# Middle attention layer of a four-layer graph network: the folds of a chunk's sums on GpSimd in place of VectorE

## The reference

```python
def _gat_layer(x, W, a_s, a_d, b, src, dst, n):
    h = x @ W
    logits = leaky_relu(h[src] @ a_s + h[dst] @ a_d, 0.2)
    m = segment_max(logits, dst, num_segments=n)
    e = exp(logits - m[dst])
    denom = segment_sum(e, dst, num_segments=n)
    coef = e / (denom[dst] + 1e-16)
    return segment_sum(coef[:, None] * h[src], dst, num_segments=n) + b
```

## Time and profile before

| what | value |
|---|---|
| median of 3 runs | 2841.45 us (2840.66 to 2842.64) |
| profiled execution, its own time | 2841.15 us |
| its span | 2838.9 us |
| TensorE busy | 2431.0 us, 86% |
| VectorE busy | 2203.5 us, 78% |
| ScalarE busy | 1548.5 us, 55% |
| GpSimd busy | 424.0 us, 15% |
| mean granted TensorE clock | 0.942 of full |

### The profile page before, as it was taken

How to read it: one execution, slowest core, us unless ns; L and a number is a source line. 1 busy time by engine, 2 the same in 40 slices (tenths; PEclk the granted TensorE clock), 3 DMA queues, 4 the chain that set the end, 5 groups by cost and what they waited for, 6 DMA issues and landing times. The chain is left out here.

```text
span 2838.9 us, 86445 instructions
## 1 busy us (share of the span) xinstructions
PE 2431.0 (86%) x31023; PEld 2188.3 (77%) x31024; DVE 2203.5 (78%) x4979; ACT 1548.5 (55%) x1943; POOL 424.0 (15%) x921
## 2 busy tenths in 40 slices
PE   2656999999999679999599998769999868999998
PEld 2644777677777569988599888669999858898997
DVE  8986899898899879999799899799999984222212
ACT  6004444444444289998799987588888740000101
POOL 1003555555556300000000000000000000000000
PEclk8877999999999889999899999989999979999999
DMA  3003443533435347676356655225655437888998
GB/s 107 0 0 87 127 127 88 166 87 108 145 87 149 99 160 266 234 265 215 104 189 205 226 181 181 91 92 183 204 181 181 158 115 247 308 306 299 330 366 299
DMA packets 398046, 494.28 MB, mean 174 GB/s; under 512 B 81925, under 2 KB 397289, under 8 KB 397674
## 3 DMA queue, kind: packets, MB, share of 16 engines
q1 hardware_dynamic: 364760, 487.44, 51.0%
q10 hardware_dynamic: 33044, 3.63, 1.0%
HBM read 401.81 MB, written 89.17 MB: 173 GB/s over the span
## 5 line engine op out<-in xcount | busy, mean ns | idle before, releaser
L2740 PE MATMUL psum<-sb_arena 128*128 128x99 bf16 (+2 forms) x13524 | 1011.3, 236 | 127.7 <-DVE sb_arena L2010 82.6
L2740 PEld LDWEIGHTS psum<-sb_arena 128*128 128x128 f16 x13524 | 969.7, 99 | 157.2 <-DVE sb_arena L2010 103.0
L3366 ACT ACTIVATE sb_arena<-sb_arena 128x896 f16 (+1 forms) x980 | 961.7, 1036 | 152.4 <-PE psum L2740 107.4
L2000 DVE TENSOR_TENSOR sb_arena<-sb_arena 128x896 f16<-128x896 f16 x980 | 593.0, 621 | 84.9 <-ACT sb_arena L3366 55.2
L3035 ACT ACTIVATE sb_arena<-psum 128x784 f16<-128x784 f32 x392 | 322.5, 823 | 394.6 <-PE psum L2385 226.5
L1280 DVE TENSOR_SCALAR sb_arena<-sb_arena 128x392 f16<-128x392 f16 x1960 | 486.9, 323 | 0.0
L2385 PE MATMUL psum<-sb_arena 64*128 64x392 f16 x3920 | 387.0, 341 | 70.1 <-ACT sb_arena L3035 25.0
L2835 PE MATMUL psum<-sb_arena 128*128 128x192 bf16 x4802 | 416.2, 248 | 30.4 <-DVEq L2157 15.2
L2835 PEld LDWEIGHTS psum<-sb_arena 128*128 128x128 f16 x4802 | 402.5, 98 | 46.0 <-DVEq L2157 16.1
L2010 DVE TENSOR_TENSOR sb_arena<-sb_arena 128x896 f16<-128x896 f16 x686 | 424.0, 618 | 0.3
L2385 PEld LDWEIGHTS psum<-sb_arena 64*128 64x128 bf16 x3920 | 258.3, 138 | 151.3 <-issue 79.8
(11 more groups left out here) (381 smaller groups left out, 1444.5 us busy)
## 6 DMA issues: line engine op xcount, KB each, us to landing
sb_arena<-counts SPq DMA_DIRECT2D x245, 896.0 KB, 6.9
sb_arena<-counts SPq DMA_DIRECT2D x245, 672.0 KB, 4.6
counts<-sb_arena SPq DMA_DIRECT2D x56, 1344.0 KB, 6.7
sb_arena<-records SPq DMA_DIRECT2D x392, 5.0 KB, 2.1
sb_arena<-records ACTq DMA_DIRECT2D x392, 5.0 KB, 2.2
counts<-sb_arena SPq DMA_DIRECT2D x1, 5488.0 KB, 19.8
records<-sb_arena SPq DMA_DIRECT2D x1, 3124.0 KB, 8.9
counts<-sb_arena SPq DMA_DIRECT2D x14, 112.0 KB, 4.6
```

The costliest lines, as they stand in the source:

```text
L2000: nc.vector.tensor_tensor(above_at[r % RING], above_at[r % RING], counts_of(g, j), ALU.mult).then_inc(above_ready, 1)
L2740: last = nc.tensor.matmul(psum[:, bank, at:at + wide], of[:, b * BLK:(b + 1) * BLK], moves[side][:, r, 0:wide], start=(r == 0 and at == 0) ...
L3366: nc.scalar.activation(above_at[r % RING], of, ACT.Sigmoid, bias=steep_s[:, r:r + 1], scale=STEEP).then_inc(signs_ready, 1)
```

## The change

GpSimd does steps 0 to 6 of the fold for the sums of chunks 0 to 5 (`fold_levels` in its own stream, the same arithmetic in 14 instructions with 9 drains), between the waits for phase 9 and phase 10, as soon as ScalarE has copied the banks out. It raises a new semaphore `folded`. VectorE no longer does these steps; in the middle layer it waits for `folded` at row MEAN_AT = 20 and does step 7 there, and step 8 at row 21. TURN_AT goes from 17 to 23, KEEP_AT from 24 to 28, MIX_AT from 26 to 30 and OUT_AT from 33 to 35. The fold of chunk 6, after the layer's end, stays whole on VectorE, and so do the folds of the first and third layers.

```diff
-TURN_AT = 17
-KEEP_AT = 24
-MIX_AT = 26
-OUT_AT = 33
+MEAN_AT = 20
+TURN_AT = 23
+KEEP_AT = 28
+MIX_AT = 30
+OUT_AT = 35
...
-                for k in range(9, 13):
-                    phase_end(pool, k)
+                def add_pieces(l, c):
...
+                    pool.wait_ge(banks_kept, c * len(groups) + (banks_before(l) + len(groups)))
+                    nc.gpsimd.tensor_tensor(kept4[:, :, 0], kept4[:, :, 0], kept4[:, :, 1], ALU.add)
+                    pool.drain()
+                    nc.gpsimd.tensor_tensor(kept4[:, :, 0], kept4[:, :, 0], kept4[:, :, 2], ALU.add)
+                    pool.drain()
+                    return kept4
...
+                def fold_levels(c):
+                    kept4 = add_pieces(1, c)
...
+                        nc.gpsimd.tensor_tensor(side, side, v.unsqueeze(2).broadcast_to([BLK, CB, wd]), ALU.mult)
+                    first, later_sums, lows = kept4[:, 0:2 * CB:2, 0], kept4[:, 1:2 * CB:2, 0], kept4[:, 2 * CB:3 * CB, 0]
+                    nc.gpsimd.tensor_scalar(picked[:, 0, :], first[:, :, fw], 0.0, None, ALU.is_gt)
+                    nc.gpsimd.tensor_scalar(picked[:, 1, :], first[:, :, fw], 0.0, None, ALU.is_equal)
+                    pool.drain()
+                    for q in range(2):
+                        nc.gpsimd.tensor_tensor(picked[:, 2 + 2 * q:4 + 2 * q, :], of_chunk(levels[:, 1 + 2 * q:3 + 2 * q, :]),
+                                                picked[:, q, :].unsqueeze(1).broadcast_to([BLK, 2, CB]), ALU.mult)
+                    scaled_by(first, of_chunk(levels[:, 0:1, :])[:, 0, :])
+                    pool.drain()
+                    nc.gpsimd.tensor_tensor(picked[:, 2:4, :], picked[:, 2:4, :], picked[:, 4:6, :], ALU.add)
+                    pool.drain()
+                    for q in range(2):
+                        scaled_by(later_sums, picked[:, 2, :])
+                        scaled_by(lows, picked[:, 3, :])
+                        pool.drain()
+                    nc.gpsimd.tensor_tensor(first, first, later_sums, ALU.add)
+                    pool.drain()
+                    nc.gpsimd.tensor_tensor(first, first, lows, ALU.add)
+                    pool.drain().then_inc(folded, 1)
+                phase_end(pool, 9)
+                fold_levels(0)
+                with pool.Fori(1, CHUNKS - 1) as c:
+                    fold_levels(c)
+                phase_end(pool, 10)
...
-                        if last and r == FOLD_AT:
+                        if l != 1 and last and r == FOLD_AT:
...
-                        elif not first and not last and 0 <= r - FOLD_AT < FOLD_STEPS[l]:
+                        elif l != 1 and not first and not last and 0 <= r - FOLD_AT < FOLD_STEPS[l]:
                             fold(c - 1, r - FOLD_AT)
+                        if l == 1 and not first and r == MEAN_AT:
+                            dve.wait_ge(folded, c)
+                            fold(c - 1, FOLD_STEPS[l] - 2)
+                        if l == 1 and not first and r == MEAN_AT + 1:
+                            fold(c - 1, FOLD_STEPS[l] - 1)
```

More of the change, by code:

```diff
@@ L614, in gnn_kernel @@
         less_ready = sem("less_ready")
+        folded = sem("folded")
         root_in = sem("root_in")
@@ L1005, in _ @@
                 last.then_inc(less_ready, 1)
-                for k in range(9, 13):
-                    phase_end(pool, k)
+                def add_pieces(l, c):
+                    groups = parts[l][7]
+                    kept4 = parts[l][3].rearrange("p q (k f) -> p q k f", k=3)
+                    if isinstance(c, int) and c == 0:
+                        pool.wait_ge(exps_ready, (l + 1) * (STEPS + 1))
+                    pool.wait_ge(banks_kept, c * len(groups) + (banks_before(l) + len(groups)))
[4 more added lines that the diff above has]
+                    return kept4
@@ new lines, in fold_levels, with of_chunk, scaled_by @@
+                def fold_levels(c):
+                    kept4 = add_pieces(1, c)
+                    fw, wd = D // 2, D // 2 + 1
+                    def of_chunk(v):
+                        return v[:, :, bass.ds(c * CB, CB)] if not isinstance(c, int) else v[:, :, c * CB:(c + 1) * CB]
+                    def scaled_by(side, v):
+                        nc.gpsimd.tensor_tensor(side, side, v.unsqueeze(2).broadcast_to([BLK, CB, wd]), ALU.mult)
[18 more added lines that the diff above has]
+                    pool.drain().then_inc(folded, 1)
@@ L1008, in _ @@
+                phase_end(pool, 9)
[3 more added lines that the diff above has]
+                phase_end(pool, 10)
+                phase_end(pool, 11)
+                phase_end(pool, 12)
             with pool.If(fast == 0):
```

## The result

The changed kernel takes 2831.3 us (median of 15 runs, 2827.0 to 2839.6) where the kernel before took 2841.1 beside it: a ratio of 0.9966, 95% interval 0.9958 to 0.9974, so 7.4 to 11.9 us less. The forecast was 2831.7.

The account below looks back on a forecast made before the run. VectorE was taken to bound rows 8 to 16 of loop chunks and all of chunk 6. Removal less GpSimd's hold gave 7.2 + 1.2 + 1.15, together 9.5 us less: about 2831.7 us, range 2818 to 2852.

Parts of the forecast that it names:

- What bounded the kernel: Middle-layer loop chunk: VectorE sets the time in rows 8 to 16; TensorE's floor is 50.8 of 56.0 us.
- What leaves VectorE: Fold steps 0 to 6 leaving VectorE: 6.3 us per loop chunk, 5.7 in chunk 1, 5.65 in chunk 6.
- What GpSimd needs: GpSimd's fold after the eviction: 10.2 us alone, done in 14 to 17, within 16.5 us before VectorE's row 20.
- The average half product: Wait ahead of each of GpSimd's 14 fold instructions beside VectorE's products: 0.27 us each, 3.8 in all.
- What GpSimd costs VectorE: GpSimd's 3059 fold elements hold up VectorE's products: 1.46 ns each, 4.5 us per fold, ends 0 and 8.0.
- Moved steps: Later reciprocal, turn, keep, mix and out cost nothing; ScalarE loses 1.7 us at the keep, covered by its lead.
- The sum: Removal less hold over six chunks: 7.2 us in the loop, 1.2 in chunk 1, 1.15 in chunk 6, together 9.5.
- GpSimd for free: First rival: GpSimd nearly free for VectorE, TensorE bounds the loop; 31 us less, 2810; chance 0.08.
- Starvation: Second rival: GpSimd gets in only at gaps, VectorE waits at row 20; 2847.7 us, chance 0.23; part-starved 0.17.
- The whole duration: Third rival: each GpSimd instruction holds VectorE for its full duration, 8.0 us per fold; 2852.7 us, chance 0.12.

Follow-up runs that it names:

- e1b: The changed kernel with fold steps 0 to 6 of chunks 0 to 5 left out, one 14-element GpSimd add kept: 2808.6 us, ratio to before 0.9891.
- e3: The changed kernel with reciprocal, means, turn, keep, mix and out back at rows 14, 15, 17, 24, 26 and 33: 2833.9 us, ratio to before 0.9976.
- e11: The changed kernel with reciprocal and means at rows 24 and 25, turn 26, keep 30, mix 32, out 35: 2842.9 us, ratio to before 1.0004.
- e9: The changed kernel with five 231-element GpSimd multiplications written as 21 of 33 elements, and the places of e11: 2857.6 us, ratio to before 1.0047.
- e12: The changed kernel with four 231-element GpSimd multiplications written as 14 of 33 elements, reciprocal and means at rows 21 and 22: 2841.6 us, ratio to before 0.9997.
- e8: The changed kernel with two more one-input GpSimd instructions of 693 elements per partition in each fold: 2841.4 us, ratio to before 0.9995.
- e4: The changed kernel with two more two-input GpSimd adds of 693 elements per partition in each fold: 2847.8 us, ratio to before 1.0026.
- e10: The changed kernel with 14 more GpSimd adds of 33 elements per fold: 2837.5 us, ratio to before 0.9987.
- e2: The kernel before, folds still on VectorE, with only the change's later places (rows 20, 21, 23, 28, 30, 35): 2845.2 us, ratio to before 1.0010.

## Why the prediction was right

**What bounded the kernel**: right. With no fold anywhere (e1b) a loop chunk is 50.4 us and TensorE's; the working gave 50.8 and put the most that a removal could bring at 5.2 us, where it is 56.24 - 50.37 = 5.87. TensorE's idle time behind VectorE was to fall from 5 us to 3.5 and fell from 3.5 to 2.1 per loop chunk; the 5 was the mean over all seven chunks, the longer chunk 6 among them.

**What leaves VectorE**: 6.3 us per loop chunk, as read from the earlier trace rows. No run tests this by itself, since e1b's loop meets TensorE's floor 5.9 us below the kernel before. In chunk 6, 5.65 was read and e1b shows 5.19; this is a mis-sized term.

**What GpSimd needs**: 14 to 17 us were forecast, 12.5 measured. The average half product ahead of each instruction was too much: GpSimd got in at the next product each time and records 11.3 us in all. That VectorE doesn't wait at row 20 is what was forecast.

**What GpSimd costs VectorE**: 4.5 us forecast, 4.2 measured, by two misses that cancel. The price per element was 1.46 ns and is 1.6 (an add of 231) to 1.77 (of 693), which would make about 5.1 us; but the first add hardly counts, since VectorE waits for row 4's sign anyway. By terms: 0.38 + 1.23 for the adds of 693, 7 x 0.37 for the seven of 231, and less than 0.1 for the five small ones. The 1.46 was read beside VectorE's TENSOR_SCALAR instructions, which have one tensor input and not two, and no row said that it would hold for products with two. That the term came out is therefore luck in part.

**Moved steps**: nothing forecast, and e3 finds nothing to regain. That ScalarE loses 1.7 us at the keep was right (1.8); e11 shows that one and two rows fewer would have made it count.

**The sum**: per loop chunk 1.77 us for 1.8. What is removed less what is held, 6.3 - 4.2 = 2.1, leaves 0.3 that shows up as idle time of VectorE behind ScalarE, such as the 0.56 at 1550.89; what makes these stays open. Chunk 1 gave 0.77 for 1.2 and chunk 6 0.91 for 1.15, so the chunks gave 8.8 for 9.5. The forecast total was met to 0.4 us although the chunks gave 0.7 less than forecast, and 1.55 us of the profiled difference lies ahead of the layer; that agreement is partly luck, within the interval of 7.4 to 11.9.

**The rivals**: GpSimd for free would be e1b's 2808.6 (2810 forecast), and isn't so. Starvation didn't occur in the changed kernel: VectorE has no idle time ahead of the reciprocal in any chunk, and in the chunk shown GpSimd was done 9 us before it. It isn't excluded in general, as e9 and e12 show with other forms of instruction. The whole duration, 11.3 us as recorded, isn't charged: VectorE lost 4.2. So the rule of the Trainium skill (SBUF — State Buffer, "SBUF: two separate sides"), by which the port pair is held for the whole instruction, agrees in that the engines exclude each other, and not in the size: by e8 and e4, what is charged is the reading.

**Where the gain comes from.** Mostly not from the large adds. In the loop of the kernel before, VectorE's first add of 693 elements and the next product:

```profile
1514.02 0.87 DVE L2057 TENSOR_TENSOR sb_arena<-sb_arena 128x693 f32<-128x693 f32 x1
1515.05 0.63 DVE L2000 TENSOR_TENSOR sb_arena<-sb_arena 128x896 f16<-128x896 f16 x1 [0.15 <-issue]
```

Done by VectorE, such an add costs it 1515.05 - 1514.02 = 1.03 us; done by GpSimd beside its products, 1.23. The pair costs 1.6 instead of 2.06 only because one lies under a wait. The other twelve instructions took some 6.3 - 2.06 = 4.2 us of VectorE and now cost 2.6. So some 0.5 of the 2.1 us comes from the pair and 1.6 from the twelve. A fold with its second large add left on VectorE wasn't tried; by these rows it would save 0.2 us per chunk, as an estimate.

## What to carry to other kernels

Work moved to GpSimd isn't free for a VectorE that runs instructions with two inputs: here it cost about 0.8 to 0.9 ns per element and input that GpSimd reads, whatever GpSimd's record says of its duration, and writes held up no product. What gained here was the short instructions, 4.2 us of VectorE for 2.6, and a large one only where VectorE waited anyway; the other large one cost 0.2 more than on VectorE. Weigh too how often an instruction has to get in between VectorE's products: 33 elements with two factors from a column took 1.62 us instead of 0.37. Then check the wait behind which the result is used, and the distances of the steps moved with it: here five rows were enough and four and three cost 1.85 us a chunk.

## What was not expected of the hardware

- An instruction of 693 elements with one input is recorded on GpSimd as 2.17 us, one with two inputs as 1.62; the first held VectorE 0.57 us, the second 1.23.
- Beside VectorE's products of 0.536 us, a GpSimd instruction of 33 elements takes 1.62 us from start to start with two factors from a column (e12), 1.08 with one (e9) and 0.58 for an add without (e10): about three, two and one products. While VectorE stands still, the one with two factors takes 0.37.
- The granted clock of TensorE in a loop chunk was 1.00 after the change and 0.97 before, with the engine busy for 52.4 of 54.6 us instead of 52.5 of 56.0. Of its two levels, 1.2 and 2.4 GHz, it now has the higher throughout such a chunk. By e2, the gain doesn't come from this.
